# Routing of a batch moved one slot later in a software-pipelined attention and expert kernel

## The reference

```python
q = rms_norm((layernorm(x) @ Wq).reshape(B, S, 16, 128), q_norm_w)
k = rms_norm((ctx @ Wk).reshape(B, S_enc, 4, 128), k_norm_w)
v = (ctx @ Wv).reshape(B, S_enc, 4, 128)
probs = softmax(einsum('bqhd,bkhd->bhqk', q, repeat(k, 4)) / sqrt(128))
x = x + einsum('bhqk,bkhd->bqhd', probs, repeat(v, 4)).reshape(B, S, 2048) @ Wo
h = layernorm(x)
rw, sel = top_k(softmax(h @ gate_w.T), 2)            # 12 experts, 2 chosen
# each expert e takes the first `cap` tokens that chose it, in order (cumsum of the choice mask)
x = x + scatter_add(rw * (silu((h @ w1[e].T) * (h @ w3[e].T)) @ w2[e].T))
```

## Time and profile before

| | value |
|---|---|
| median of 3 runs | 2662.54 us (2662.12 to 2664.76) |
| the profiled execution, its own time | 2652.94 us |
| its span | 2651.2 us |
| PE / PEld busy | 2422.2 us (91%) / 1875.8 us (71%) |
| DVE busy | 2082.9 us (79%) |
| ACT busy | 1646.5 us (62%) |
| POOL busy | 1112.9 us (42%) |
| mean DMA rate | 125 GB/s |

### The profile page before, as it was taken

The page is one execution under the profiler, slowest core; times in us unless marked ns, Lnnn a source line. Parts: engine busy times, 40 slices in busy tenths (PEclk is TensorE's granted clock), DMA queues, the critical chain, the costliest instruction groups (busy, mean ns, idle before and its releaser), DMA issues. The chain is left out here.

```text
span 2651.2 us, 51686 instructions
## 1 busy us (share of the span) xinstructions
PE 2422.2 (91%) x12985; PEld 1875.8 (71%) x12985; DVE 2082.9 (79%) x5478; ACT 1646.5 (62%) x4789; POOL 1112.9 (42%) x1279
## 2 busy tenths in 40 slices
PE   3899999999999999999999999999999999749883
PEld 3777777777777777777777777777777777525451
DVE  5688888888888888888888888888888878737552
ACT  4566766666666666666666666666666666515441
POOL 0334334343433443434333344344343434258885
PEclk8999999999999999999999999999999999969875
DMA  7455555555555555555555555555555545449997
GB/s 214 84 118 118 122 125 119 125 117 120 127 118 118 116 119 127 119 123 120 118 127 120 120 115 117 126 121 121 123 118 124 123 105 113 97 116 189 182 180 98
DMA packets 778098, 331.20 MB, mean 125 GB/s; under 512 B 695340, under 2 KB 707884, under 8 KB 778032
## 3 DMA queue, kind: packets, MB, share of 16 engines
q1 hardware_dynamic: 754960, 287.61, 48.8%
q0 software_dynamic: 22912, 43.16, 9.1%
q10 hardware_dynamic: 192, 0.04, 0.0%
HBM read 108.15 MB, written 57.71 MB: 63 GB/s over the span
## 5 line engine op out<-in xcount | busy, mean ns | idle before, releaser
L904 ACT CAST pt_hi<-work 128x512 fp32r<-128x512 f16 x256 | 158.9, 621 | 617.9 <-DMA work<-work 617.9
L890 ACT ACTIVATE work<-pb,small 128x128 f32<-128x128 f32 x1024 | 454.5, 454 | 27.4 <-DVE small L1034 27.4
L716 PE MATMUL pb<-wq_hi,x_hi 128*128 128x512 f32 x1024 | 408.8, 399 | 32.2 <-POOL x_lo L1265 22.4
L787 PE MATMUL pb<-wo_hi,ot_hi 128*128 128x512 f32 x1024 | 413.7, 404 | 3.2 <-DVE ot_lo L970 3.0
L716 PE MATMUL pb<-wq_lo,x_hi 128*128 128x512 f32 x1024 | 401.4, 392 | 0.0
L716 PE MATMUL pb<-wq_hi,x_lo 128*128 128x512 f32 x1024 | 401.1, 392 | 0.0
L787 PE MATMUL pb<-wo_lo,ot_hi 128*128 128x512 f32 x1024 | 401.0, 392 | 0.0
L787 PE MATMUL pb<-wo_hi,ot_lo 128*128 128x512 f32 x1024 | 400.4, 391 | 0.0
L1288 POOL TENSOR_TENSOR small<-small 128x4 f32<-128x4 f32 x256 | 155.8, 609 | 544.7 <-DVE small L1016 544.7
L1022 DVE SCALAR_TENSOR_TENSOR work<-pb,small,work 128x128 f16<-128x128 f32 x1024 | 286.7, 340 | 45.1 <-ACT work L880 45.1
L880 ACT ACTIVATE work<-pb,small 128x128 f16<-128x128 f32 x1024 | 291.3, 366 | 0.0
(11 more groups left out here) (144 smaller groups left out, 5297.6 us busy)
## 6 DMA issues: line engine op xcount, KB each, us to landing
work<-x SPq DMA_DIRECT2D x128, 256.0 KB, 3.2
work<-cT SPq DMA_DIRECT2D x64, 256.0 KB, 2.8
work<-xT SPq DMA_DIRECT2D x64, 256.0 KB, 3.2
out<-work SPq DMA_DIRECT2D x64, 256.0 KB, 4.7
xn_scratch<-work SPq DMA_DIRECT2D x64, 256.0 KB, 2.0
work<-work SPq DMA_TRANSPOSE x640, 3.3
work<-wq SPq DMA_DIRECT2D x16, 256.0 KB, 3.1
work<-wo SPq DMA_DIRECT2D x16, 256.0 KB, 3.5
```

The source lines that it names most:

```text
L716: mm = nc.tensor.matmul(bank[:, :], lhs[a][:, c, :], rhs[b_][:, c, :], start=(c == 0 and n == 0), stop=(c == NC - 1 and n == 2))
L787: mm = nc.tensor.matmul(WO_B[:, :], otp[a][:, h, :], wop[b_][:, g * HPG + h, :], start=(g == 0 and h == 0 and n == 0), stop=(g == NG - 1 a ...
L890: ex = nc.scalar.activation(probs[:, cols], S_B[:, cols], ACT.Exp, bias=nmax[:, h:h + 1], scale=esc, accum_out=psums[:, h:h + 1])
L904: nc.scalar.copy(ptp[0][:, :, :], pT16[:, HI, :]).then_inc(pt_hi, 1)
```

## The change

`route`, `copy_logits` and `choose` of batch b-2 move from slot 1 to slot 2. With them the conditions on the shared bank move: `attend` waits for the copied logits in group 1 and no longer in group 0, and `route` waits for one more unit of `ot_lo`. `exp_diff` goes from slot 2 to the end of slot 3. On DVE `norm_k` stays in slot 2 but goes from ahead of `normalise` to the end of the slot; `split_k` goes from the end of slot 2 into slot 3, on both ACT (ahead of `exps`) and DVE (ahead of `norm2` and `normalise`). Nothing is added or removed. The new file has one line more, so every line from 768 on reads one higher in it.

```diff
@@ PE @@
                     if g == 0:
                         wait(pe, v_lo, b + 1)
+                    if g == 1:
                         wait(pe, lg_cp, b - 1)
...
                 def route(b):
                     wait(pe, d_xT, 16 * (b + 1))
-                    wait(pe, ot_lo, min(4 * b + 8, NU) if isinstance(b, int) else 4 * b + 8)
+                    wait(pe, ot_lo, min(4 * b + 9, NU) if isinstance(b, int) else 4 * b + 9)
...
-                        if g == 1 and live(b - 2):
+                        if g == 2 and live(b - 2):
                             route(b - 2)
@@ ACT @@
-                        if g == 2 and live(b - 2):
-                            exp_diff(b - 2)
+                        if g == 3 and live(b + 1):
+                            split_k(b + 1)
                         if live(b):
                             exps(*cur)
...
-                        if g == 2 and live(b + 1):
-                            split_k(b + 1)
+                        if g == 3 and live(b - 2):
+                            exp_diff(b - 2)
@@ DVE @@
-                        if g == 2 and live(b + 1):
-                            norm_k(b + 1)
+                        if g == 3 and live(b + 1):
+                            split_k(b + 1)
                         if g == 3 and live(b - 1):
                             norm2(b - 1)
                         if live(b):
                             normalise(*cur)
-                        if g == 1 and live(b - 2):
+                        if g == 2 and live(b - 2):
                             copy_logits(b - 2)
...
-                        if g == 1 and live(b - 2):
+                        if g == 2 and live(b + 1):
+                            norm_k(b + 1)
+                        if g == 2 and live(b - 2):
                             choose(b - 2)
                         if g == 2 and live(b - 1):
                             stats_2(b - 1)
-                        if g == 2 and live(b + 1):
-                            split_k(b + 1)
```

## The result

| | before | changed |
|---|---|---|
| median of the runs | 2662.33 us (4 runs, 2659.89 to 2664.76) | 2699.23 us (4 runs, 2697.49 to 2700.49) |
| ratio | | 1.0138, 95% interval 1.0121 to 1.0156 |
| span of the profiled execution | 2651.2 us | 2698.8 us |

What follows compares the result with a forecast made beforehand. The prediction took a closed round of the probabilities through ACT, DVE and SP as the limit, not PE. -0.70 + 1.27 = +0.57 us a batch, times 61 = 35 us, on the 2662.54 median gives 2697.5 us; range 2680 to 2712.

Steps and rivals of the forecast that it cites:

- The round: Closed path `split_p`, `turn_p`, `widen_p`, `exps`, `normalise`, `split_p` through DVE, SP and ACT; four turns make the 34.82 us batch.
- `choose` out of slot 1 and `norm_k` out of the way of `normalise`: Between P1 and P2: `exps` of slot 2 starts 0.61 us earlier, `normalise` gains 0.09; together 0.70 us a batch gained.
- P1: Start of DVE's `split_p` in slot 1, from which times in the following stretch are counted.
- What fills the end of slot 2: DVE from P2 to slot 3's maxima: `norm_k` and `choose` in, `split_k` out, 4.25 to 5.56 us; 1.27 us a batch lost.
- P2: Start of DVE's `split_p` in slot 2, from which times up to slot 3 are counted.
- `split_k` covered ahead of `normalise` in slot 3: DVE's 0.58 us of `split_k` fits its 0.62 idle there; at most 0.05 left over, `exps` to `split_p` stays 3.49.
- Keys late, at no cost: Turned keys land at P2 + 10.6, so slot 0's scores wait on PE, at no cost to the round.
- PE as the limit: First of three rivals: PE sets the pace, `route` no longer waits, 0.45 us a batch gained, 2635 us; chance 0.06.
- ACT as the limit of slot 3: Rival: ACT, not DVE, sets `exps` of slot 3 at P2 + 5.12; 0.10 to 0.17 us a batch gained, about 2654; chance 0.09.
- Late keys as a bound: Rival: `turn_k` lands later, behind other transfers; 1 us beyond the free room gives 61 more, 2758 us; chance 0.05.
- P3: Start of DVE's `split_p` in slot 3, from which times into slot 0 are counted.
- The ends: First two batches without `choose`, last ones without keys: counted as no change, bounded by 1 to 2 us either way.

Runs made afterwards that it cites:

- e5: Kernel before without the low part of the context in keys and values, 8 matmuls less in a batch on PE: 2660.32 us, ratio 1.0002.
- e6: Kernel before with two more 128x128 ACT instructions in slot 1, between `widen_p` and `exps`, written where nothing reads: 2679.32 us, ratio 1.0071.
- e9: Kernel before with `split_xn2` (slot 0) and `split_v` (slot 1) ahead of `widen_p` on ACT: 2609.24 us, ratio 0.9804.
- e2: Changed kernel with `split_k` back at the end of slot 2 on ACT and DVE: 2725.78 us, ratio 1.0277 against the kernel before.
- e3: Changed kernel with `stats_2` moved on DVE from the end of slot 2 to ahead of `normalise`: 2642.74 us, ratio 0.9968 against the kernel before.
- e1: Changed kernel with `norm_k` back ahead of `normalise` in slot 2: 2681.99 us, ratio 1.0114 against the kernel before.
- e7: Kernel before with only `route`, `copy_logits`, `choose` and `exp_diff` moved; `norm_k` and `split_k` left where they were: 2701.98 us, ratio 1.0181.
- e10: Changed kernel with `norm_k` back ahead of `normalise` and, on POOL, `rms_k` ahead of `scatter` in slot 1: 2656.18 us, ratio 1.0012 against the kernel before.
- e8: Changed kernel with `stats_2` ahead of `normalise` (DVE) and `split_k`, `split_xn2`, `split_v` ahead of `widen_p` (ACT): 2591.19 us, ratio 0.9745 against the kernel before.

## Why the prediction was right

*The round sets the pace, not PE.* Right, and shown from three sides: 8 matmuls less in a batch change nothing (e5), 0.32 us more on an ACT that idles cost 0.33 us in its slot (e6), and the order of ACT's casts alone gives 50 us (e9).

*`choose` out of slot 1 and `norm_k` out of the way of `normalise`, -0.70 us.* Measured -0.69 (8.71 to 8.02). `exps` of slot 2 started at P1 + 4.53 in the median, predicted 4.51.

*What fills the end of slot 2, +1.27 us.* Measured +1.31 (8.02 to 9.33), the upper of the two values given; the negated maxima came at P2 + 5.57, predicted 5.56. I had taken the middle between one batch's 1.24, in which a late transfer had already held `exps` up, and 1.31. Over the batches it was 1.31. That is the whole difference between 0.57 and 0.61 us a batch, and 61 x 0.61 = 37 us is the measured difference of the medians. That the two agree to a tenth is luck, as the paragraph on the ends shows.

*`split_k` covered ahead of `normalise` in slot 3.* Right: `exps` to `split_p` stayed at 3.49.

*Keys late, at no cost.* Right: PE waits 0.3 us before the scores (0.7 us by its weight loads), and removing this wait gains nothing (e2). The output projection that was to wait in slot 3 waits in slot 1 instead; in slot 3 it is `positions`, which stands ahead of it.

*The rivals.* PE as the limit is ruled out by e5. ACT as the limit of slot 3 did not come about, but e3 produces it by taking 0.87 us from DVE's passage, and it costs what was worked out (slot 2 to 3 of 8.52; P2 + 5.12 + 3.49 = 8.61 by the rows of one batch). Late keys as a bound did not occur. Its "another 1.5 us or so" rests on no row; in the trace of before the negated maxima of slot 0 come at P3 + 2.98 and `exps` starts at P3 + 5.51, which leaves about 2.3 us (5.51 - 2.98 - 0.27), so that late keys would have had to be later still. Of the first rival one part is borne out: it said that 0.62 of PE's 1.07 us would stay as a wait for `ot_lo`, and 0.63 did.

*What I had not seen.* `norm_k` has a second condition, POOL's `rms_k`, which ends at P1 + 6.05. The prediction did not need it, because the change moves `norm_k` behind that point; my expectations of e1 and e7 did, and were off by 0.4 us a batch. The prediction's account of the old slot 2 (DVE was just finishing `norm_k`) was right, but POOL held it just as tightly: in e7 DVE comes 0.85 us earlier and `norm_k` still starts at P1 + 6.09, before at P1 + 6.08. e10 shows that it comes free when the root goes first.

*The ends.* Left at nothing. In the profiled executions the last `split_p` lies 35.8 us later in the changed kernel, the first 0.8 us, so the stage grew by 35.0 us and not by 37. The first three batches add 2.2 us to the pattern, the last one takes 0.5 off. One thing inside did not belong to the steady pattern: in the kernel before, one batch, the 60th, took 39.3 us. The waits between 2130 and 2200 us show it:

```profile
POOL token_table L1303 <- issue: 5.1, 4, 4.5
...
DVE work L997 <- POOL small L1280: 4.1, 1, 4.1
```

POOL issued one of its indirect transfers 4.5 us late, `rms_k` stood behind it, and `norm_k` behind that. In the changed kernel, whose `norm_k` comes later, no batch past the third takes over 0.7 us more than the median. Such a batch, 4.4 to 5.5 us over the median, is also there in e1, e5, e6, e7 and e9, which all have `norm_k` early behind `scatter`, and not in e2 and e3, which have it late; in e8 (late) and e10 (root first) it is 0.9 us over. So the change has one small gain, some 4 us once.

The last stage, the experts, took 341.0 us from the last `split_p` in the profile of before and 352.8 in that of the changed kernel, though nothing in it changed. Over the eleven profiles it varies from 339 to 353 us without regard to the edit. The spans of two profiles therefore differ by 47.6 us where the medians differ by 36.9. What the last stage adds to the medians is not known, and the difference is known only to within 32 to 42 us; the firm test of the prediction is the ruler above, 0.61 us a batch against 0.57.

## What to carry to other kernels

A wait on the busiest engine is worth something only if what it waits for is not itself paced by a closed round on other engines. Follow one item round until you are back at the same instruction one turn later, and check whether each step starts when the one before ends; if it does, that round is the limit, however idle its engines look. In such a pipeline an instruction's price depends on its place first: work put ahead of a wait of the round was free (e9, 2.0%), the same work behind it costs up to its full time, until the other branch of the round is the later one (`split_v` behind `widen_p` takes 0.48 us of ACT, and moving it gave 0.28). A move is costed by the gap that it leaves as well as by the one that it fills. Before crediting an instruction with an earlier start, list every semaphore that it waits for, with the queue behind each; a condition that is met just in time shows in no list of waits.

## What the runs showed of the hardware

Two ACT instructions of 128x128 from PSUM with a constant scale followed each other at 0.16 us each (0.32 for two), four with a scale that differs by row at 0.25 to 0.26 us each (1.02 for four); the cause of the difference was not tested. And among the 128 indirect transfers that `scatter` issues on POOL, the 114th started late in all eleven profiled executions, by 3.2 us in e10 and 4.5 to 5.1 us in the ten others, while the others in the steady stretch followed within 0.3 us. What POOL does there the traces do not say, and it was not tested.
